# A graph kernel on one core: new order of its last pair, other blocks of M, narrow opening products, and a last tile in two halves

## The reference, cut to what matters

```python
# x: (32, 256, 512), adj: (256, 256), four weights (512, 512), all float32
z_l, z_g, v = x @ W_lang.T, x @ W_grav.T, x @ W_V.T
zn  = z_l / max(norm(z_l), EPS)
A_l = max(zn @ zn.T, 0) * not_eye
A_g = exp(-max(sq + sq.T - 2 * z_g @ z_g.T, 0) / (2 * sigma**2)) * not_eye
K   = w_l * row_normalised(A_l * adj) + (1 - w_l) * row_normalised(A_g * adj)
out = layernorm(x + (K @ v) @ W_O.T)        # over the last axis
```

## Time and profile before

| | |
|---|---|
| median of 3 runs | 654.11 us (653.62 to 655.98) |
| the profiled execution | 655.62 us, its span 653.9 us |
| PE busy | 641.2 us, 98% |
| DVE, ACT, POOL busy | 533.6, 383.4, 136.1 us |
| DMA | 106.48 MB, 163 GB/s over the span |
| PE's share of the chain that ended last | 92% |

### The profile page before, as it was taken

The page is one execution under the profiler, slowest core; times in us unless marked ns, Lnnn a source line. Parts: engine busy times, 40 slices in busy tenths (PEclk is TensorE's granted clock), DMA queues, the critical chain, the costliest instruction groups (busy, mean ns, idle before and its releaser), DMA issues.

```text
span 653.9 us, 10726 instructions
## 1 busy us (share of the span) xinstructions
PE 641.2 (98%) x2858; PEld 530.1 (81%) x2858; DVE 533.6 (82%) x1430; ACT 383.4 (59%) x707; POOL 136.1 (21%) x288
## 2 busy tenths in 40 slices
PE   8999999999999999999999999999999999999995
PEld 7888888888888888888888888888888888887774
DVE  5774979798897978888797978979797988978785
ACT  5453545656665565657556565756656566555665
POOL 2711011211211121121212112121211112112022
PEclk9999999999999999999999999999999999999999
DMA  9311757484665749386575928566683847454542
GB/s 294 76 54 51 176 160 175 119 246 104 210 158 174 197 134 246 85 256 140 165 177 174 226 80 259 127 193 150 186 209 111 250 104 229 109 167 140 161 136 106
DMA packets 141509, 106.48 MB, mean 163 GB/s; under 512 B 40112, under 2 KB 115632, under 8 KB 141488
## 3 DMA queue, kind: packets, MB, share of 16 engines
q1 hardware_dynamic: 140768, 104.40, 57.5%
q0 software_dynamic: 288, 1.05, 0.5%
q10 hardware_dynamic: 432, 0.79, 0.3%
HBM read 65.80 MB, written 40.40 MB: 162 GB/s over the span
## 4 chain that ended last, share of the span: by engine, by line
PE 92%; DVE 3%; DMA 2%; SPq 1%; ACT 1%; issue 1%; DVEq 0%; ACTq 0%
PE bank L1397 58%; PE bank L1485 17%; PE bank L1490 14%; PE bank L1442 2%; DMA work<-k_spill 1%; DVE p_lo L1033 1%; SPq L439 1%; DMA x_spill<-xs 1%; DMA r_row<-r_spill 1%; DMA xs<-in_L_gnn_W_lang 1%; PE bank L1420 0%; DVE work L1091 0%; DVE work L1148 0%; PE bank L1423 0%; SPq L422 0%
## 5 line engine op out<-in xcount | busy, mean ns | idle before, releaser
L735 ACT ACTIVATE p_hi<-bank,m_scale 128x512 fp32r<-128x512 f32 x128 | 85.8, 683 | 54.5 <-PE bank L1490 53.5
L1033 DVE SCALAR_TENSOR_TENSOR p_lo<-bank,m_scale,p_hi 128x512 fp32r<-128x512 f32 x128 | 94.0, 747 | 18.6 <-ACT p_hi L735 18.6
L1490 PE MATMUL bank<-hT_lo,m_hi 128*128 128x512 f32 x384 | 107.8, 389 | 0.0
L1397 PE MATMUL bank<-wvo_hi,hT_hi 128*128 128x512 f32 x256 | 99.7, 389 | 0.0
L1397 PE MATMUL bank<-wvo_hi,hT_lo 128*128 128x512 f32 x256 | 99.6, 389 | 0.0
L1397 PE MATMUL bank<-wvo_lo,hT_hi 128*128 128x512 f32 x256 | 99.6, 389 | 0.0
L1397 PE MATMUL bank<-p_hi,hT_hi 128*128 128x512 f32 x256 | 99.6, 389 | 0.0
L1397 PE MATMUL bank<-p_lo,hT_hi 128*128 128x512 f32 x256 | 99.6, 389 | 0.0
L608 POOL TENSOR_TENSOR rnorm<-norm,minus_half 128x2 f32<-128x2 f32 x32 | 34.8, 1088 | 245.1 <-DVE norm L1061 245.1
L1490 PEld LDWEIGHTS bank<-hT_lo,m_hi 128*128 128x128 f32 x384 | 72.1, 188 | 15.0
L739 ACT CAST v_hi<-bank 128x512 fp32r<-128x512 f32 x60 | 32.4, 590 | 62.6 <-PE bank L1397 62.6
(11 more groups left out here) (163 smaller groups left out, 1253.6 us busy)
## 6 DMA issues: line engine op xcount, KB each, us to landing
x_blk<-in_x SPq DMA_DIRECT2D x128, 128.0 KB, 3.5
x_spill<-xs SPq DMA_DIRECT2D x30, 512.0 KB, 3.8
xq<-x_spill SPq DMA_DIRECT2D x120, 128.0 KB, 3.5
x_nat<-in_x SPq DMA_DIRECT2D x30, 512.0 KB, 4.5
out_y<-y SPq DMA_DIRECT2D x30, 512.0 KB, 4.1
k_spill<-work SPq DMA_DIRECT2D x30, 256.0 KB, 2.2
work<-k_spill SPq DMA_DIRECT2D x120, 64.0 KB, 2.3
r_row<-r_spill SPq DMA_DIRECT2D x32, 128.0 KB, 3.5
```

Source lines behind the costliest of these rows:

```text
L735: nc.scalar.activation(p_hi[:, :, j, g, :], src[:].rearrange("p (b n) -> p b n", b=2), ACT.Copy, scale=m_scale[:, g, j:j + 1]).then_inc(pr ...
L1033: nc.vector.scalar_tensor_tensor(out=p_lo[:, :, j, g, :], in0=src[:].rearrange("p (b n) -> p b n", b=2), scalar=m_scale[:, g, j:j + 1], in ...
L1397: last = pe.matmul(dst, lhsT, rhs, start=(n == 0), stop=(n == len(steps) - 1))
L1490: last = pe.matmul(pbank(k)[:], md_hi[:, g, 0] if i == 0 else m_hi[:, g, i, c], lo[i], start=False, stop=(i == DT - 1))
```

## The change

1. **Opening**: only `kt_hi[:, 0, 0, 0]` (128 columns) is zeroed, and `WARM = 35` products of 128 columns take the place of six of 512.
2. **Blocks of M**: row 0 makes all four blocks, and rows 1 to 3 two blocks each (row 1: 1 and 3; row 2: 1 and 2; row 3: 2 and 3). The blocks (1,0), (2,0), (3,0), (3,1), (1,2) and (2,3) are turned over from their mirror images, two for each `MIRROR` unit. A mirror unit now waits for the hi part of row 3 of its M. `project` uses the made blocks' scaled lo part where `made(i, j)` says so.
3. **The last pair**: a new order on SP, ACT, DVE, POOL and PE.
4. **The very last tile** (1,1): PE makes it as 12 products of 256 columns into two banks; DVE adds x to each half (`end_residual`) and sums the halves (`end_mean`); DVE scales half 0 (`end_scale`) and SP stores it, ACT scales half 1 (`end_normalise`) and stores it from its own queue.

```diff
+        def made(i, j):
+            return (i, j) in ((0, 1), (0, 2), (0, 3), (1, 3), (2, 1), (3, 2))
...
+        def end_bank(h):
+            return (last_kv_bank(1, NT - 1), pbank(2 * DT + 2))[h]
...
-        WARM = 6
+        WARM = 35
...
+            spread_r(q, 1)
             return_x(q, 1)
-            spread_r(q, 1)
             spill_k(q, 0)
+            return_k(q, 0)
+            load_x(q, 0)
+            spill_k(q, 1)
+            store(q - 1, 0)
+            return_k(q, 1)
+            store_r(p, 0)
             load_last(0)
             load_x(q, 1)
-            spill_k(q, 1)
-            return_k(q, 0)
-            load_x(q, 0)
-            store(q - 1, 1)
-            return_k(q, 1)
-            store(q - 1, 0)
-            store_r(p, 0)
             spread_r(p, 0)
             store_r(p, 1)
+            store(q - 1, 1)
+            spread_r(p, 1)
             load_last(1)
-            spread_r(p, 1)
             store(q, 0)
-            store_last(0, 1)
             store(q, 1)
             store_last(0, 0)
-            store_last(1, 1)
+            store_last(0, 1)
+            sp.wait_ge(last_normed[1][1], 1)
+            sp.dma_start(half_of(out_v[2 * p + 1][:, 1], 0), half_of(last_x(1)[:, 1], 0)).then_inc(last_stored, 16)
...
-            nc.gpsimd.memset(kt_hi[:, 0].bitcast(F32), 0.0).then_inc(warm_ready, 1)
+            nc.gpsimd.memset(kt_hi[:, 0, 0, 0].bitcast(F32), 0.0).then_inc(warm_ready, 1)
...
@@ scalar
+            proj_hi_part(p, 0)
+            proj_hi_part(p, 1)
             squares(q - 1, 0)
-            proj_hi_part(p, 0)
-            squares(q - 1, 1)
-            proj_hi_part(p, 1)
+            proj_hi_part(p, 2)
             gauss(q, 1)
...
+            save_x(p, 0, 0)
             proj_hi_part(p, 8)
             save_x(p, 0, 1)
+            centre(p, 0)
             kt_hi_part(q, 0)
             save_x(p, 1, 0)
             save_x(p, 1, 1)
+            last_gauss(0)
+            centre(p, 1)
+            normalise(q - 1, 1)
             kt_hi_part(q, 1)
...
@@ vector
+            gauss_masked(q, 0)
             gram(q, 0, L)
+            proj_lo_part(p, 0)
             turn_x(q, 1)
             cosine_masked(q, 0)
             gram(q, 1, G)
             proj_lo_part(p, 1)
+            proj_lo_part(p, 2)
+            row_factors(q, 0)
+            gram(q, 1, L)
+            proj_lo_part(p, 3)
+            inverse_masked(q, 1)
+            proj_lo_part(p, 4)
...
@@ tensor
                 elif kind == MIRROR:
-                    pe.wait_ge(prep_lo, prepared(UPPER, g, i - 1))
-                    for r in range(i):
+                    pe.wait_ge(prep_hi, prepared(UPPER, g, DT - 1))
+                    for r in [r for r in range(DT) if made(r, i)]:
...
-                pe.matmul(kv_bank[1][:], kt_hi[:, 0, 0, 0], in_kt(kt_hi, 0), start=True, stop=True)
+                pe.matmul(kv_bank[1][:, 0:P], kt_hi[:, 0, 0, 0], kt_hi[:, 0, 0, 0], start=True, stop=True)
...
+                if is_end(b, t):
+                    for h in range(2):
+                        products(end_bank(h)[:, 0:D // 2],
+                                 [(lhsT, half_of(rhs, h)) for lhsT, rhs in steps]).then_inc(last_out[b], 1)
...
+            last_gram_turn(p, 0, G)
             last_gram_turn(p, 0, L)
             k_times_v(q, 0, 0)
             k_times_v(q, 0, 1)
-            last_gram_turn(p, 0, G)
             last_gram_turn(p, 1, G)
             last_gram_turn(p, 1, L)
             value(p, 1, 0, 1)
+            k_times_v(q, 1, 0)
+            k_times_v(q, 1, 1)
             pe.wait_ge(last_gram[0][L], 1)
             value(p, 1, 1, 0)
-            k_times_v(q, 1, 0)
             last_k_turn(p, 0)
-            k_times_v(q, 1, 1)
             pe.wait_ge(last_gram[0][G], 1)
             value(p, 1, 1, 1)
+            last_k_times_v(p, 0, 0)
             last_k_turn(p, 1)
-            last_k_times_v(p, 0, 0)
             last_k_times_v(p, 0, 1)
```

More of the change, by code:

```diff
@@ L139, in diagonal_blocks, with row_blocks, mirrored_blocks @@
             return (flat[:, 0:(DT - 1) * step].rearrange("p (i w) -> p i w", w=step)[:, :, 0:P], flat[:, (DT - 1) * step:])
+        def made(i, j):
+            return (i, j) in ((0, 1), (0, 2), (0, 3), (1, 3), (2, 1), (3, 2))
+        def row_blocks(row, i):
+            if i == 0:
+                return row
+            if i == 1:
+                return row.rearrange("p (k two n) -> p k two n", two=2, n=P)[:, :, 1]
+            return row[:, (i - 1) * P:(i + 1) * P]
+        def mirrored_blocks(tile, i):
+            row = tile.rearrange("p (k n) -> p k n", n=P)
+            if i == 1:
+                return row.rearrange("p (a two) n -> p a two n", two=2)[:, :, 0]
+            return row[:, 0:2] if i == 3 else None
         def split_blocks(tile, g):
@@ L698, in prep_hi_part @@
                 if kind == MIRROR:
[L699 removed]
+                    if i == 2:
+                        for j in (0, DT - 1):
+                            c = slice(j * P, (j + 1) * P)
+                            last = nc.scalar.copy(m_hi[:, g, i, c], src[:, c])
+                    else:
+                        last = nc.scalar.copy(mirrored_blocks(m_hi[:, g, i], i), mirrored_blocks(src[:], i))
+                    last.then_inc(mirrored, 1)
                     return
                 if kind == UPPER:
[L702 removed]
+                    nc.scalar.copy(row_blocks(m_hi[:, g, i], i), row_blocks(src[:], i)).then_inc(prep_hi, 1)
                 else:
@@ L860, in last_squares, with end_normalise @@
                                      accum_out=last_rstd[:, b, t:t + 1]).then_inc(last_sq_ready[b][t], 1)
+            def end_normalise():
+                b, t = 1, NT - 1
+                act.wait_ge(last_shift_ready[b][t], 1)
+                half = half_of(last_x(b)[:, t], 1)
+                nc.scalar.activation(half, half, ACT.Identity, bias=last_shift[:, b, t:t + 1],
+                                     scale=last_rstd[:, b, t:t + 1]).then_inc(end_half, 1)
             def last_normalise(b, t):
@@ L1435, in prepare @@
                 elif kind == UPPER:
-                    cols = slice(i * P, D)
-                    steps = three_products(rows, w_parts[g], w_parts[g], cols)
+                    hi, lo = w_parts[g]
+                    steps = [s for k in range(DT)
+                             for s in ((hi[:, k, rows], row_blocks(hi[:, k], i)), (hi[:, k, rows], row_blocks(lo[:, k], i)),
+                                       (lo[:, k, rows], row_blocks(hi[:, k], i)))]
                     for n, (lhsT, rhs) in enumerate(steps):
@@ L1558, in last_k_times_v @@
                     steps += [(hi, last_v(m_hi, b, u)), (hi, last_v(m_lo, b, u)), (lo, last_v(m_hi, b, u))]
-                products(last_kv_bank(b, t)[:], steps).then_inc(last_out[b], 1)
+                if is_end(b, t):
+                    for h in range(2):
+                        products(end_bank(h)[:, 0:D // 2],
+                                 [(lhsT, half_of(rhs, h)) for lhsT, rhs in steps]).then_inc(last_out[b], 1)
+                else:
+                    products(last_kv_bank(b, t)[:], steps).then_inc(last_out[b], 1)
             def k_times_v(q, b, t):
```

122 lines of the change are left out of this document (69 added, 53 removed).

## The result

The changed kernel takes **653.03 us** (median of 16 runs, 652.08 to 653.89) beside 654.52 us for the kernel before on the same chip (16 runs, 653.61 to 656.46): a ratio of 0.9972, 95% interval 0.9962 to 0.9981, so 1.5 us (the medians) to 1.8 us (0.28% of 654.5) faster. Forecast were 648.0 us and a range of 645.3 to 651.5; the result lies outside, at the place of the rival "the narrow products do not lift the clock" (652.3).

A forecast was written before the change was run, and what follows sets the result against it. PE, busy 98% of the span, was taken as the bound, with gains only where it waits or runs slowly: 0.7 + 0.8 + 3.1 + 1.5 = 6.1 us, from 654.1 to 648.0 us; range 645.3 to 651.5.

The forecast's parts named there:

- the narrow products do not lift the clock: Opening, rival at 12%: 35 products at 0.215 us end at 8.5, first block at 13.6; -3.6 for 0.7, so 652.3 us.
- Part 1: The opening: narrow products at 0.18 us, clock up at 4.9, first block over at about 9.3; 0.7 us won.
- the rival that it gave: Opening, rival at 15%: columns alone set the narrow products' price at the lower clock; 2.1 us for 0.7, so 646.6 us.
- Part 2: Blocks of M: 256-column rows save 0.5 us for L and 0.65 for G, mirror wait costs 0.35; 0.8 us won.
- Part 3: The last pair: new orders remove PE's three stalls, 3.5 us to be had less 0.4 for a new one; 3.1 won.
- The new one named in advance: Last pair: DVE's lo part ends at 640.05 where PE wants it at 639.7; 0.4 us lost with restart.
- Part 4: The end: last tile in halves and `store(q, 1)` leaving earlier shorten the stretch behind PE's last product; 1.5 us won.
- The halves bring nothing: The end, rival at 12%: one store's latency, not bandwidth, sets the end; 0.2 us gained there, so 649.3 us.

## Why the prediction was wrong, and where it was right

**Part 1 failed, at two steps.** The first is the price: "I take 0.18" at the lower level; it is 0.215, the upper bound given there (twice the upper level's price), with the weight load at 332 ns. The rule of the Trainium skill that the prediction weighed ("TensorE: Matmul & The Clock Gate", section "Wait — 56ns, not 53.3ns?", N / 1.2 ns, 107 ns for 128 columns) did not hold here: the runs show twice that for these float32 products with a load each, and the rival that it gave fell with it. This step alone would have cost little: with 0.215 and the clock still up at 4.9, 18 products are done by then and the other 17 end at 6.7, not 6.5. The second, larger one is "I choose the time at which the weights' own products used to begin, 4.9" for the clock's rise, a choice without a row under it. The products were still slow after 7.5 us of narrow ones, and stayed so up to 13.5, well into the wide ones. The 7.95 that the prediction gives as its best end of the block has no working either (4.7 and 2.7 make 7.4), and the 2.1 us of the rival hang on it.

How 3.68 us come out of that: the first block starts at 8.61 where it started at 4.89, 3.72 later, and takes 13.73 - 8.61 = 5.12 us where it took 10.05 - 4.89 = 5.16. It ran at the lower level for nearly all of its length both times. The whole loss is the late start: an opening that is twice as long and brings nothing. Seventeen narrow ones, which end at 4.86, cost nothing against six wide ones (0.9913 and 0.9923) and win nothing that can be told.

The rival's 12% was too low. Its argument ("products of zeros and short; no row shows that such ones lift it") was half right, short and not zeros. The one row that spoke to it, six wide products of 2.9 us that had not lifted the clock, was put aside with their small number. With no row for the forecast's own step, the two deserved nearly equal chances, and the range should have reached 652.3 and a little further. The rival forecast 652.3, and the measurement says 653.0. Of these 0.7 us, 0.4 lie in the base (654.11 when the forecast was made, 654.52 over 16 runs), and 0.3 in a gain of 1.5 us and not 1.8. The ledger has a gain of 2.2, for its terms were read off one profiled execution, of 655.62 us, which stands 1.1 us above the median of the 16 runs of the kernel before, while that of the changed kernel, 653.48, stands 0.45 above its own. The openings of the profiles with six wide products end at 10.05, 10.16, 10.15, 9.71, 8.46 and 7.96. That the typical opening of the kernel before ends earlier than the 10.05 of the ledger fits this, but no run shows it.

**Part 2 right** (0.8 forecast, 0.69 measured, 0.55 in the pair of profiles with six wide). Rows 1 to 3 of L went from 4.82 to 18.04 - 13.73 = 4.31, the 0.5 of the forecast. The mirror's wait was 0.56 and not 0.35. What the forecast didn't have is POOL: where three or four reductions of DVE fall beside its subtractions, PE waits 1.3 or 2.4 us, and part 2 brings nothing. ACT's cast took its 0.37, as the timeline shows, but starts about 0.2 behind the last product:

```profile
27.86 0.37 ACT L744 CAST m_hi<-bank 128x256 fp32r<-128x256 f32 x1 [0.89 <-PE bank L1520]
...
28.38 0.41 PE L1525 MATMUL bank<-ident,m_hi 128*128 128x128 f32 x2 [0.56 <-ACT m_hi L744]
```

**Part 3 right** (3.1 forecast, 3.49 and 3.55 measured). All three stalls of the earlier trace rows are gone. The new one named in advance came at its place, ahead of `last_kt_lo_part(1)`, but on PEld (0.5 us in the waits) with PE itself still fed: PE stands still for 46.33 - 46.23 = 0.1 us, so nearly all of the 3.5 was had. The moved `store(q - 1, 1)` went out at 628.69, 11 us later than in the earlier trace rows, and starved nobody.

**Part 4 right in size** (1.5 forecast, 1.55 measured) and in its reason: the drain of `store(q, 1)` was the bound, and it is worth 1.3. "The halves bring nothing" put the whole of part 4 at 0.2 for that case; the halves do bring next to nothing, and the end shrinks all the same. The forecast had not split the two; the kernels with the whole last tile did.

## What to carry to other kernels

If TensorE is to be warmed, use wide products (256 or 512 columns here) and end them when the first data is there: a filler that goes on past it is paid in full, and one of narrow products may lift nothing. How much a better filler wins over six wide products the times here don't tell. When an unmeasured step decides the sign, give its rival the chance that the missing row leaves it. And look at the order of the queues first: 4.9 us of this kernel's gain cost no instruction at all, and one store moved ahead of another was worth more than a tile cut in two.

## What the runs showed of the hardware that was not expected

- **At 1.2 GHz a float32 product of 128 columns costs as much as one of 256**: 0.213 us both, by the start times, and 0.427 for 512. At 2.4 GHz they are 0.107, 0.119 and 0.227. So something other than columns sets the price of the narrow ones. The weight load is the likely cause (PEld is busy through the whole opening, 332 ns a load), but no run separates it from another fixed cost of a product.
- **35 narrow products in 7.5 us left the clock low; behind 18 of 256 columns, in 3.9 us, it had risen**, and behind nine of 512 the first fast product starts at 5.8 and 7.0 us. With the same opening the rise comes at different times from one profile to the next (block ends of 7.96 to 10.16 with six wide products, 12.37 to 13.73 with 35 narrow ones).
- **The granted clock reads 1.00 in the opening** while products come at 0.43; the spacing of like products is the thing to read there.
- **A reduction of DVE that reads two tiles from SBUF takes up to 1.38 us and not 0.29 beside POOL's subtraction.** It is in the changed kernel too. Its timelines of POOL and of DVE:

```profile
19.22 2.62 POOL L602 TENSOR_TENSOR v_lo<-xq,v_hi 128x512 fp32r<-128x512 f32 x2 [11.30 <-ACT v_hi L727]
22.93 2.54 POOL L602 TENSOR_TENSOR v_lo<-xq,v_hi 128x512 fp32r<-128x512 f32 x2 [1.09 <-ACT v_hi L727]
```

```profile
19.32 1.38 DVE L1015 CUSTOM_DVE_ANT_0 x_nat<-m_lo,ident 128x128 f32<-128x128 f32 x1
...
23.68 0.43 DVE L1003 TENSOR_TENSOR m_lo<-bank,m_hi 128x256 fp32r<-128x256 f32 x1 [0.23 <-ACT m_hi L744]
24.50 0.69 DVE L1007 TENSOR_TENSOR hT_lo<-bank,hT_hi 128x512 fp32r<-128x512 f32 x1 [0.40 <-ACT hT_hi L747]
```

The reduction starts 0.1 behind POOL's first subtraction, which is over at about 20.5, and ends at 20.7, while POOL keeps its 1.3 a piece. The splits, which have one input in a PSUM bank, run beside the second pair of subtractions at their usual 0.43 and 0.69. The page "SBUF — State Buffer" of the Trainium skill, section "Who interferes with whom", says that a DVE instruction with two SBUF inputs contends with a GpSimd instruction that reads SBUF, that one with at most one doesn't (outside certain modes with two ports), and that the ports the two engines share are locked by one of them at a time. These rows agree: the reduction, which came second, takes as long as the subtraction that it met, and the splits don't. POOL's subtraction didn't wait for DVE in any of the rows shown here; the stretched side was DVE's.
